# Flamingo block with MoE on one core: routing slots, GpSimd scaling, expert order and bank waits changed together

## The reference, cut to what matters

```python
x = x + tanh(g_xattn) * attention(layernorm(x), ctx)     # x: 16 x 112 x 512, ctx: 16 x 375 x 128
x = x + tanh(g_ffn)   * moe(layernorm(x))

def attention(xn, ctx):                                  # 16 heads
    q    = rope((xn @ Wq.T).heads @ w_kc_q)              # 384 wide, per head
    kv   = rope(ctx)
    attn = softmax((q @ W_qr) . (kv @ W_kr))
    return ((attn @ kv) @ w_kc_kv).joined @ Wo.T

def moe(xn):                                             # 1792 tokens, 64 experts, top 8
    topv, topi = top_k(xn @ gate_w.T, 8)
    w   = softmax(topv)
    out = sum over the 8 of w * (silu(gate_e(xn)) * up_e(xn)) @ dp_e
    return out + sigmoid(xn @ sh_gate1.T) * shared_expert(xn)
```

## Time and profile before

| | |
|---|---|
| median of 3 runs | 1828.55 us (1826.33 to 1829.11) |
| the profiled execution | 1830.79 us, its span 1828.7 us |
| granted TensorE clock, mean | 0.921 |
| PE busy | 1468.3 us (80%) |
| DVE busy | 1242.9 us (68%) |
| ACT busy | 755.9 us (41%) |
| POOL busy | 817.4 us (45%) |
| HBM read, written | 218.90 MB, 67.61 MB |

### The profile page before, as it was taken

How to read it: one execution, slowest core, us unless ns; L and a number is a source line. 1 busy time by engine, 2 the same in 40 slices (tenths; PEclk the granted TensorE clock), 3 DMA queues, 4 the chain that set the end, 5 groups by cost and what they waited for, 6 DMA issues and landing times.

```text
span 1828.7 us, 24620 instructions
## 1 busy us (share of the span) xinstructions
PE 1468.3 (80%) x7484; PEld 1177.9 (64%) x7484; DVE 1242.9 (68%) x2658; ACT 755.9 (41%) x1706; POOL 817.4 (45%) x800
## 2 busy tenths in 40 slices
PE   4689898888789988879897887888659889999700
PEld 4377687666568766658776665756348778888600
DVE  2177785377778358779827777766447677877577
ACT  1123585111178311128721114745138667776500
POOL 1078432155544025663303565202357777777500
PEclk9989999999899999899999899999769999999955
DMA  7977201344310234430033441121168899999798
GB/s 191 315 233 238 87 14 36 106 135 140 98 46 5 64 119 133 134 91 20 5 94 115 141 127 29 36 66 53 54 196 260 285 313 329 313 313 302 245 424 350
DMA packets 140410, 285.98 MB, mean 156 GB/s; under 512 B 29422, under 2 KB 64840, under 8 KB 138184
## 3 DMA queue, kind: packets, MB, share of 16 engines
q1 hardware_dynamic: 112328, 212.39, 35.9%
q0 software_dynamic: 25344, 64.69, 10.6%
q10 hardware_dynamic: 2608, 7.34, 1.3%
HBM read 218.90 MB, written 67.61 MB: 157 GB/s over the span
## 4 chain that ended last, share of the span: by engine, by line
PE 43%; DVE 22%; DMA 11%; issue 9%; ACT 7%; POOL 5%; SPq 1%; DVEq 0%; ACTq 0%; POOLq 0%
PE bank L598 11%; PE bank L600 10%; PE bank L599 10%; DVE q_sin L976 4%; PE bank L676 4%; DMA p_in<-parts 4%; DVE q_rope L972 3%; POOL parts L1600 3%; ACT prob L1332 3%; DMA w_dp<-in_w_dp 2%; DMA parts<-y_sb,t_rows 2%; PE bank L743 2%; POOL x_g L1593 2%; PE bank L701 1%; PE bank L792 1%
## 5 line engine op out<-in xcount | busy, mean ns | idle before, releaser
L1534 POOL TENSOR_TENSOR q_rope<-q_rope,q_sin 128x448 f32<-128x448 f32 x192 | 214.5, 1146 | 209.7 <-DVE q_sin L976 209.7
L1540 POOL TENSOR_SCALAR prob<-prob,row_inv 128x375 f32<-128x375 f32 x100 | 123.7, 1237 | 171.9 <-DVE row_inv L998 171.8
L676 PE MATMUL bank<-q_rope,m_w 128*128 128x448 f32 x384 | 164.8, 567 | 25.0 <-DVE q_tl L982 21.9
L1600 POOL DMA_INDIRECT parts<-y_sb,t_rows x140 | 152.3, 1088 | 50.3 <-issue 37.5
L1593 POOL DMA_INDIRECT x_g<-xn_dram,t_rows x140 | 144.0, 1028 | 54.0 <-issue 37.5
L1553 POOL DMA_INDIRECT table<-entry,pos_i x128 | 121.5, 949 | 91.1 <-DVE pos_i L1091 44.6
L976 DVE TENSOR_TENSOR q_sin<-bank,sin_q 128x448 f32<-128x448 f32 (+1 forms) x256 | 158.4, 619 | 3.9
L990 DVE TENSOR_REDUCE row_max<-bank 128x1 f32<-128x375 f32 x224 | 119.6, 535 | 23.8 <-PE bank L600 23.4
L1332 ACT ACTIVATE prob<-bank,row_max 128x375 f32<-128x375 f32 x224 | 132.1, 590 | 8.6 <-DVE row_max L990 8.6
L701 PE MATMUL bank<-ident,prob 128*125 128x128 f32 x672 | 115.5, 282 | 19.9 <-DVE prob_t1l L1011 6.6
L676 PEld LDWEIGHTS bank<-q_rope,m_w 128*128 128x128 f32 x384 | 73.9, 197 | 83.1 <-issue 81.9
(11 more groups left out here) (277 smaller groups left out, 4580.6 us busy)
## 6 DMA issues: line engine op xcount, KB each, us to landing
w_gu<-in_w_gu SPq DMA_DIRECT2D x64, 512.0 KB, 4.8
p_in<-parts SPq DMA_DIRECT2D x14, 2304.0 KB, 13.0
v_raw<-v_dram SPq DMA_DIRECT2D x80, 256.0 KB, 2.7
w_dp<-in_w_dp SPq DMA_DIRECT2D x64, 256.0 KB, 6.2
m_w<-m_dram SPq DMA_DIRECT2D x64, 192.0 KB, 2.6
wq_s0h<-wq_dram SPq DMA_DIRECT2D x24, 256.0 KB, 3.3
wq_s0l<-wq_dram SPq DMA_DIRECT2D x24, 256.0 KB, 3.9
wq_s1h<-wq_dram SPq DMA_DIRECT2D x24, 256.0 KB, 2.9
```

The source lines that it names most:

```text
L676: m = pe.matmul(bank[5][:, 0:GT], m_w[n % NW][:, c, :], q_rope[h % 2][:, c, :], start=(c == 0), stop=(c == QC - 1))
L1534: pool.tensor_tensor(o[:, c, :], o[:, c, :], q_sin[:, c, :], ALU.add).then_inc(s_radd, 1)
L1600: pool.indirect_dma_start(parts, bass.IndirectOffsetOnAxis(ap=t_rows[x % NROW][0:size, t, 1:2].bitcast(I32), axis=0), y_sb[x % NY][t][0:si ...
```

## The change

1. `SLOTS` and the period change: norm stays in its batch's slot 0, turn is in slot 4, router 6, choose 7, rank 9, place 10, shared and scatter low 11, scatter high 12; batch i starts at slot 7 * i. TensorE's waits for bank 7 and bank 6 follow. SyncE does its stores `STORE_LAG` = 4 slots later.
2. All tiles that ScalarE or GpSimd scaled are scaled by GpSimd, with `tensor_tensor` and the reciprocal as a broadcast column in place of `tensor_scalar`; the second half of the last group stays shared by ScalarE and VectorE.
3. The order is computed inside `END`, after the last batch's place, without waiting for the scatters. SyncE loads three experts' weights as soon as the order is there, and the rows after `wait_attention_over`. TensorE and VectorE no longer wait there, ScalarE only for the last `s_route`; the first weights are split before the first rows are turned.
4. `inner(x)` waits for bank 3 and for bank 4 apart.

```diff
-SLOTS = (0, 1, 3, 4, 6, 7, 8, 9, 11)
+SLOTS = (0, 4, 6, 7, 9, 10, 11, 11, 12)
+PERIOD, STORE_LAG = 7, 4
...
-    return [(step, (g - 1) * GB + i) for i in range(GB) for at, step in zip(SLOTS, STEPS) if 8 * i + at == slot]
+    return [(step, (g - 1) * GB + i) for i in range(GB) for at, step in zip(SLOTS, STEPS) if PERIOD * i + at == slot]
...
-       + [(s, B2, 5) for s in STEPS[3:]])
+       + [(s, B2, 5) for s in STEPS[3:6]] + [("order", B2, 5)] + [(s, B2, 5) for s in STEPS[6:]])
...
 def scaled_by(n):
-    if n % 2 == 0:
-        return "act"
     g, t = n // (GB * RT), n % (GB * RT) + 2
-    return "dve" if g == NG - 1 and HALF <= t else "pool"
+    if g == NG - 1 and HALF <= t:
+        return ("act", "dve")[n % 2]
+    return "pool"
...
             for step, b, _ in END:
                 finish(step, b)
+            sp.wait_ge(s_order, 1)
+            for x in range(NE):
+                load_expert(x)
             wait_attention_over(sp)
-            sp.wait_ge(s_order, 1)
             for x in range(NROW_AHEAD):
                 load_rows(x)
-                if x < NE:
-                    load_expert(x)
...
             def router_in(b, bk):
                 pe.wait_ge(s_x2t, b + 1)
+                if 0 < b < B - GB:
+                    pe.wait_ge(s_route, NR * b)
...
                     elif b == B - GB:
                         pe.wait_ge(s_kt_lo, B - 1)
+                    elif b < B - GB:
+                        pe.wait_ge(s_route, NR * (b - 1) + R_RANKED)
...
+                if step == "order":
+                    pe.wait_ge(s_route, NR * b + R_COUNT)
+                    pe.matmul(bank[3][0:E, 0:E], count[:], ones[:, 0:E], start=True, stop=True)
+                    pe.matmul(bank[3][0:E, E:2 * E], ones[:, 0:E], count[:], start=True, stop=True).then_inc(s_total, 1)
+                    pe.wait_ge(s_ranked, 5)
+                    pe.matmul(bank[4][0:E, 0:E], number[:], at_place[:], start=True, stop=True)
+                    pe.matmul(bank[4][0:E, E:2 * E], total[:], at_place[:], start=True, stop=True).then_inc(s_total, 1)
...
-                if x:
-                    pe.wait_ge(s_inner, 4 * (x - 1) + 2)
                 for bk, at in ((3, 0), (4, I)):
+                    if x:
+                        pe.wait_ge(s_inner, 4 * (x - 1) + (1 if bk == 3 else 2))
...
-            wait_attention_over(act)
+            act.wait_ge(s_route, NR * B)
...
+            split_expert(0)
             turn(0)
-            split_expert(0)
...
-                    pool.tensor_scalar(prob[i][:], prob[i][:], row_inv[:, i:i + 1], None, ALU.mult)\
+                    pool.tensor_tensor(prob[i][:], prob[i][:], row_inv[:, i:i + 1].to_broadcast([P, L]), ALU.mult)\
```

More of the change, by code:

```diff
@@ L515, in sync @@
                         reload_wcq(n + 1)
-                    for step, b in between(g, 2 * h):
+                    for step, b in between(g, 2 * h - STORE_LAG):
                         finish(step, b)
@@ L519, in sync @@
                         load_mw(g * H + h - 2 + NW)
-                    for step, b in between(g, 2 * h + 1):
+                    for step, b in between(g, 2 * h + 1 - STORE_LAG):
+                        finish(step, b)
+                for slot in range(2 * (H + 2) - STORE_LAG, 2 * (H + 2)):
+                    for step, b in between(g, slot):
                         finish(step, b)
@@ L1108, in finish @@
                     place(b)
+                if step == "order":
+                    dve.wait_ge(s_total, 1)
+                    dve.tensor_copy(total[:], bank[3][0:E, 0:E]).then_inc(s_ranked, 1)
+                    dve.tensor_tensor(key_own[:], bank[3][0:E, 0:1], lower_own[:], ALU.add).then_inc(s_ranked, 1)
+                    dve.tensor_tensor(key[:], bank[3][0:E, E:2 * E], lower_first[:], ALU.add).then_inc(s_ranked, 1)
+                    dve.wait_ge(s_ranked, 3)
+                    dve.tensor_scalar(above[:], key[:], key_own[:], 0.0, ALU.is_gt, ALU.add, accum_out=place_of[:])\
+                       .then_inc(s_ranked, 1)
+                    dve.wait_ge(s_ranked, 4)
+                    dve.tensor_scalar(at_place[:], expert[0:E, :], place_of[:], None, ALU.is_equal).then_inc(s_ranked, 1)
+                    dve.wait_ge(s_total, 2)
+                    dve.tensor_copy(order[:], bank[4][0:1, 0:E]).then_inc(s_order, 1)
                 if step == "shared":
@@ L1190, in vector @@
                 finish(step, b, bk)
-            wait_attention_over(dve)
-            dve.wait_ge(s_total, 1)
-            dve.tensor_copy(total[:], bank[5][0:E, 0:E]).then_inc(s_ranked, 1)
-            dve.tensor_tensor(key_own[:], bank[5][0:E, 0:1], lower_own[:], ALU.add).then_inc(s_ranked, 1)
-            dve.tensor_tensor(key[:], bank[5][0:E, E:2 * E], lower_first[:], ALU.add).then_inc(s_ranked, 1)
-            dve.wait_ge(s_ranked, 3)
-            dve.tensor_scalar(above[:], key[:], key_own[:], 0.0, ALU.is_gt, ALU.add, accum_out=place_of[:])\
-               .then_inc(s_ranked, 1)
-            dve.wait_ge(s_ranked, 4)
-            dve.tensor_scalar(at_place[:], expert[0:E, :], place_of[:], None, ALU.is_equal).then_inc(s_ranked, 1)
-            dve.wait_ge(s_total, 2)
-            dve.tensor_copy(order[:], bank[6][0:1, 0:E]).then_inc(s_order, 1)
-            dve.tensor_tensor(excess[:], bank[6][0:1, E:2 * E], caps[:], ALU.subtract).then_inc(s_rounds, 1)
+            dve.tensor_tensor(excess[:], bank[4][0:1, E:2 * E], caps[:], ALU.subtract).then_inc(s_rounds, 1)
             dve.wait_ge(s_rounds, 1)
```

11 lines of the change are left out of this document (2 added, 9 removed).

## The result

The changed kernel takes 1779.16 us, median of 4 runs (1772.12 to 1785.47), against 1827.57 for the kernel before beside it: ratio 0.9734, 95% interval 0.9688 to 0.9779. It is faster; 1770 was forecast, in a range of 1742 to 1806. Its profiled execution took 1785.47 us, with a span of 1783.7, 45.0 less than before.

What follows compares the result with a forecast made beforehand. TensorE was taken to pace the heads, engines in lockstep the score tiles, GpSimd the experts. Heads 45, tiles 7, order 6 and banks 1 sum to 59 us off 1828.55, giving 1770 us, range 1742 to 1806.

Steps and rivals of the forecast that it cites:

- The three waits and the one that stays: Heads: of TensorE's four stalls for VectorE's norm three go, 19.4 us a group; the first stays in another form.
- The double scatter: Heads: both scatter halves in one head make GpSimd's adds late, 3.2 us of TensorE stall plus up to 1.56 of clock.
- The wait for place: Heads: the turn must wait until place has read its ranks, 0.4 us each in two of three cases, 0.8 a group.
- VectorE and TensorE owe the same 27 us a period: Heads: per 3.5-head period VectorE owes 25.9 to 27 us, TensorE 26.9, so VectorE's lag can reach TensorE.
- The lock on the context rotation: Score tiles: GpSimd's scaling may hold VectorE's context rotation 0.2 to 0.77 us in each of 14 batches, 3 us.
- Rival C: Score tiles: GpSimd's scaling at 2.0 us becomes the bound and the kernel is slower, 1861 us; chance 0.06.
- SyncE is not in the chain here: 0: SyncE's queue: moving the stores two heads later was priced at no gain or loss.
- Less about 1: Hand-over to the experts: 2.3 MB of early weights share DMA engines with the last scatters, about 1 off 6.7 us.
- my reason for 1: Experts: per-bank waits spare TensorE at most 10 us, but GpSimd, waiting only 11.3 us for y_sb, sets the pace.
- A (heads only passed on, 24): Heads: the stall is only passed on, so they give 24 and not 45, 1791 us; chance 0.23.
- B (25 from the tiles): Score tiles: ScalarE was the true bound, so they give 25 instead of 7, 1752 us; chance 0.13.
- D: Heads: norm is early but the turn waits for place and the bank comes late; heads give nothing, 1815 us; chance 0.05.

Runs made afterwards that it cites:

- f_turn5: The changed kernel with the turn one slot later (5 instead of 4), on chip B: 1851.1 us, ratio 0.975 to the kernel before.
- f_mask: The changed kernel with the mask made by comparing the logits with the eighth value, on chip B: 1854.61 us, ratio 0.9764 to the kernel before.
- g_mask: The changed kernel with the mask made by a comparison that also writes its sum per row, on chip C: 1780.14 us, ratio 0.9721 to the kernel before.
- e_scale: The kernel before with only GpSimd's new-form scaling of all tiles but those of the last pass, on chip A: 1886.15 us, ratio 0.9906.
- g_all: The changed kernel with late weights, turn at slot 5 and the mask with its sum, on chip C: 1777.53 us, ratio 0.9718 to the kernel before.
- e_slots: The kernel before with only the new slots, TensorE's two waits and the lag of SyncE's stores, on chip A: 1870.47 us, ratio 0.9822.

## Why the prediction was right, and where not

Direction, size and order of the terms held; the sum was 59, and the profiles show 45 (the medians 48). Part of the fit is luck: in the tiles a gain that was too small and a loss that was not forecast cancel.

*Heads, 45 forecast, 38.3 measured* (12.7 off the forecast's 154 is 141 a group, where 139 was to show it right and 148 wrong). The three waits and the one that stays were right; so was 6.6 at the end. The items given back were the mis-sized step: 4.5 a group was forecast, 19.4 - 12.8 = 6.6 was measured. The double scatter cost 0.7 us of direct wait, not 3.2. The wait for place cost 2.4, not 0.8, but f_turn5 shows that taking it away brings nothing. What I did not price is the choice beside GpSimd's adds: 1.81 + 1.36 us a group, with scatters in front of the adds. The prediction had both halves, late adds behind scatters, and VectorE held by GpSimd, but put the second on the context rotation (0.2 to 0.77 us) and never laid the two on one another; they met at choose, in two of four batches at the mask and in a third, behind the double scatter, for 3.9 us. None of f_mask, g_mask and f_turn5 freed VectorE of the holds as a whole: f_turn5's are longer at the mask (2.9 to 3.2 us). That all three leave the heads at 153 fits "VectorE and TensorE owe the same 27 us a period" better than any single wait: that remains argued, not shown.

*Tiles, 7 forecast, 6.0 measured, right only as a sum.* The scaling alone gives 12 (e_scale) and not 7. The instruction takes 0.81 us, and I took 1.0 from rows with two full operands, so my price was too high by a fifth. The lock on the context rotation, for which I had taken 3 off, isn't there: the rotation's longest operation takes 557 to 559 ns in all sixteen batches, before and after. Rival C had its turning point at 1.84 us and is out. So is the estimate of 1.79 us from the Trainium skill's GPSIMD Engine Reference ("Elementwise — side-by-side cycle accounting"): by this trace the form with a second operand is the cheaper one here. Against the 12 stand some 5 that the slots cost the tiles beside the new scaling (groups 1 and 2 take 97.8 and 97.6 us, 96.0 and 95.9 in e_scale), and 8 where they stand alone. The step that failed is "SyncE is not in the chain here: 0": the lag of the stores makes the load of x late, VectorE waits 2.8 to 3.2 us for it in the changed kernel, GpSimd's scaling waits for VectorE, and the clock falls to 0.83. I had put 3 for a later start by the scatters, and nothing for the load or the clock.

*Order and weights, 6 forecast, 0.4 measured with the banks* (2.6 up to the first put). The order did come early, but what SyncE waits for is the landing of the last scatter, and with the weights asked for early that took 5.85 us, not 3.28 as with late ones (g_all), after its issue; the 3 us that were to show the forecast right did not come. "Less about 1" for the shared DMA engines was the step that failed: it costs 2.6, nearly all of the 2.9 that the early order was to bring. The gaps before gathers went (3.8 us), and the first put came 2.5 us sooner after the first gather (1318.46 - 1293.43 = 25.0; before 1365.24 - 1337.68 = 27.6), 3.02 us of wait at that put included, where it was 1.07 before. From first put to last it then takes 366.5 us, before 364.4, and that is where 2.1 went again. It isn't GpSimd's waits for y_sb, 10.4 us there and 10.2 before; and since the same stretch spreads from 362.5 to 366.5 in this profile and the three on C, it may be no more than that spread. On chips A and B, where the experts are slower, asking early costs 7 to 9 us.

*Banks, 1 forecast, no gain to be seen here*, 9 by the medians and 15 by the profiles on chip A, above my upper end of 6. The bound was not the arithmetic of the wait but whose pace the experts keep: on a chip where GpSimd waits 87.6 us, my reason for 1 does not hold.

*Rivals.* A (heads only passed on, 24) lost: 38.3 against its 24. B (25 from the tiles) lost: the scaling alone gives 12, and ScalarE freed waits 11.6 us for the row maximum in the third group's tiles instead. D did not happen.

## What to carry over

A freed wait is worth what the next two queues leave of it: before an operation is moved, look not only at what it waits for but at what runs on GpSimd in the slot where it will stand. Work asked for early on a queue shared with a landing that everybody waits for is not free; ask behind it. A store that is moved back moves every load that waits for its buffer: follow that load to the first engine that needs it before writing 0. And name the engine that sets the pace of a stage on more than one chip before writing down a change of another engine as nothing.

## What the runs showed that I had not expected

- GpSimd's tensor_tensor with a broadcast column takes 812 ns for 128 x 375 (2.2 ns a column), its tensor_scalar with a column per partition 1237 (3.3), its tensor_tensor with two full operands 1278 for 512 columns (2.5).
- VectorE's tensor_tensor of two SBUF tensors, tensor_scalar with one, and cast with one were each held for 2.0 to 2.5 us by GpSimd's three adds in the changed kernel, f_mask and g_mask, up to 3.2 with the turn at 5, and a one-column tensor_tensor for 3.9; the compare that also writes its sum (0.28), the maximum, the index search and the replacement just ahead of it, and operations that read PSUM were not.
- Two of the chips take 60 to 90 us longer behind the last row maximum; before it they differ by 3 to 7 us, in the last group's tiles. In the experts of these chips ScalarE stands up to 4.2 us before its tanh with nothing of its own core as the releaser (18 times, 59.2 us, in e_slots), and SyncE pauses between weight loads. The granted clock over the experts is 0.88 in e_slots (1308 to 1789) and 0.96 in the changed kernel (1291 to 1696). What causes it stays open.
